# Self-attention on one core: the next queries' projection, the output projections and the norms in another order

## What is computed

```python
def _attn(xq, xc, Wq, Wk, Wv, Wo, bo):
    q = (xq @ Wq).reshape(B, N, HEADS, D_HEAD)      # 16 heads of 64
    k = (xc @ Wk).reshape(B, S, HEADS, D_HEAD)
    v = (xc @ Wv).reshape(B, S, HEADS, D_HEAD)
    scores = jnp.einsum('bnhd,bshd->bhns', q, k) * scale
    attn = jax.nn.softmax(scores, axis=-1)
    out = jnp.einsum('bhns,bshd->bnhd', attn, v).reshape(B, N, HEADS * D_HEAD)
    return out @ Wo + bo
...
x = _attn(_ln(x, g1, b1), _ln(x, g1, b1), Wq1, Wk1, Wv1, Wo1, bo1) + x
```

## Time and profile before

| | |
|---|---|
| median of 3 runs | 2309.28 us (2304.2 to 2310.44) |
| span of the profiled execution | 2302.8 us, 31305 instructions |
| self-attention in it, about | 571 to 1750 us |
| busy in the span | PE 92%, PEld 77%, DVE 70%, ACT 64%, POOL 46% |
| matmuls, 128x512, `mm3` | L146, L147, L148, 2944 each |
| exponentials L1500 | 256, mean 1027 ns |
| maxima L1588 | 256 of 1214 ns |

### The profile page before, as it was taken

The page is one execution under the profiler, slowest core; times in us unless marked ns, Lnnn a source line. Parts: engine busy times, 40 slices in busy tenths (PEclk is TensorE's granted clock), DMA queues, the critical chain, the costliest instruction groups (busy, mean ns, idle before and its releaser), DMA issues. The chain is left out here.

```text
span 2302.8 us, 31305 instructions
## 1 busy us (share of the span) xinstructions
PE 2128.1 (92%) x11628; PEld 1775.1 (77%) x11628; DVE 1608.6 (70%) x2345; ACT 1482.6 (64%) x2154; POOL 1070.1 (46%) x819
## 2 busy tenths in 40 slices
PE   7867999987799999999999999999998799999998
PEld 4656888876677778777777777777776689888987
DVE  5576676664677787777877778778776866666553
ACT  5546877754677777777777777777774345454431
POOL 2154444432245454454544545445444665656432
PEclk9989999999999999999999999999999999999999
DMA  6810000010100100100001000000004411111000
GB/s 219 290 40 4 22 22 21 10 67 28 33 24 15 33 15 15 38 15 24 24 15 33 15 24 29 15 33 15 24 26 152 144 46 56 56 56 47 10 10 19
DMA packets 84281, 102.67 MB, mean 45 GB/s; under 512 B 29665, under 2 KB 61153, under 8 KB 83617
## 3 DMA queue, kind: packets, MB, share of 16 engines
q1 hardware_dynamic: 84128, 100.66, 13.2%
HBM read 65.50 MB, written 33.82 MB: 43 GB/s over the span
## 5 line engine op out<-in xcount | busy, mean ns | idle before, releaser
L146 PE MATMUL PS<-R 128*128 128x512 f32 (+1 forms) x2944 | 1028.1, 349 | 84.0 <-DVE R L162 54.8
L148 PE MATMUL PS<-R 128*128 128x512 f32 (+1 forms) x2944 | 997.6, 339 | 0.0
L147 PE MATMUL PS<-R 128*128 128x512 f32 (+1 forms) x2944 | 997.3, 339 | 0.0
L146 PEld LDWEIGHTS PS<-R 128*128 128x128 f32 x2944 | 566.4, 192 | 197.5 <-DVE R L162 64.0
L156 ACT ACTIVATE R<-PS 64x512 fp32r<-64x512 f32 (+4 forms) x860 | 460.1, 548 | 238.7 <-PE PS L1805 129.4
L148 PEld LDWEIGHTS PS<-R 128*128 128x128 f32 x2944 | 565.7, 192 | 61.1
L147 PEld LDWEIGHTS PS<-R 128*128 128x128 f32 x2944 | 567.6, 193 | 54.8
L162 DVE TENSOR_TENSOR R<-F,R 128x1024 fp32r<-128x1024 f32 (+2 forms) x416 | 466.1, 1126 | 46.5 <-POOL R L159 23.2
L159 POOL TENSOR_SCALAR R<-F 128x1024 fp32r<-128x1024 f32 (+1 forms) x295 | 263.8, 896 | 292.6 <-DVE F L1958 149.3
L1500 ACT ACTIVATE F<-PS 128x1024 f32<-128x1024 f32 x256 | 263.0, 1027 | 172.7 <-DVE R L162 115.2
L159 POOL TENSOR_SCALAR R<-R 64x512 fp32r<-64x512 f32 x128 | 143.0, 1132 | 392.5 <-ACT R L156 392.4
(11 more groups left out here) (89 smaller groups left out, 1992.1 us busy)
## 6 DMA issues: line engine op xcount, KB each, us to landing
F<-sd SPq DMA_DIRECT2D x128, 128.0 KB, 2.8
xs<-F SPq DMA_DIRECT2D x16, 512.0 KB, 2.6
F<-xs SPq DMA_DIRECT2D x16, 512.0 KB, 3.6
gd<-F SPq DMA_DIRECT2D x8, 768.0 KB, 4.0
vd<-F SPq DMA_DIRECT2D x8, 768.0 KB, 6.3
R<-gd SPq DMA_DIRECT2D x6, 1024.0 KB, 5.6
R<-vd SPq DMA_DIRECT2D x6, 1024.0 KB, 5.7
F<-in_x SPq DMA_DIRECT2D x8, 512.0 KB, 5.4
```

The source lines that it names most:

```text
L146: nc.tensor.matmul(o, L[0], Rr[0], start=start, stop=False, skip_group_check=share)
L147: nc.tensor.matmul(o, L[0], Rr[1], start=False, stop=False, skip_group_check=share)
L148: return nc.tensor.matmul(o, L[1], Rr[0], start=False, stop=stop, skip_group_check=share)
```

## The change

Eight things are written in another place:

- `project(u + 1, 0)` stands in quarter 3 behind `values(d, 3)`, ahead of the transposes; it no longer waits for `o3_add`, since nothing else writes bank 2 behind the maxima. Only the very first one stays in quarter 0.
- `values(d, 0)` stands where `project(u, 0)` was, between the two parts of the first scores.
- `output(e, 0)` goes to bank 7 and stands behind the transposes, with a wait for all four maxima of the unit; `output(e, 1)` stays in bank 7, with a wait for the addition of half 0. The last pair keeps banks 4 and 5.
- On VectorE the probability rest of quarter 3 stands ahead of the addition of half 0.
- The load of the next batch's x, its statistics (`p = 3`), its scale and GpSimd's power (`p = 4`), and its transposes, weights and split (`p = 5`) all stand one unit earlier. GpSimd's `ln_add` stays behind `p = 5`.

```diff
--- before.py
+++ after.py
@@ -1272,7 +1272,7 @@
 
         def out3_bank(e, half):
 
-            return (4, 5)[half] if e == N3 - 1 else (2, 7)[half]
+            return (4, 5)[half] if e == N3 - 1 else 7
 
         def odd_bank(u):
 
@@ -1324,7 +1324,7 @@
                         sp_values(0)
                     for _ in range(early4.get(at, 0)):
                         next(ahead)
-                if ok(s, N3) and p == 3:
+                if ok(s, N3) and p == 2:
                     if b + 1 == NB:
                         sp_bias(3)
                     sp_load(*after3(b), xs)
@@ -1357,8 +1357,6 @@
                 pe.wait_ge(ln_nl, 17 + b)
                 wait_weights(pe, "q1", "k1")
                 pe.wait_ge(b3_max, 4 * (u - 1) + 2)
-                if n == 0:
-                    pe.wait_ge(o3_add, last_o3(u - 4))
                 for k in range(2):
                     m = mm3(bank(2 + n), [v[:, k, 128 * p:128 * p + 128] for v in (W3q, W3k)[n]],
                             [v[:, k, :] for v in ns[b % 2]], k == 0, k == 1)
@@ -1416,16 +1414,16 @@
             for s in loop3:
                 t, u, d = s, s + 1, s - 1
                 b, p = divmod(max(t, 0), 8)
-                norm = ok(t, N3) and p == 6
+                norm = ok(t, N3) and p == 5
                 for j in range(4):
                     if ok(t, N3):
                         scores(t, j, 0)
-                    if ok(u, N3) and j == 0:
+                    if u == 0 and j == 0:
                         project(u, 0)
+                    if ok(d, N3) and j == 0:
+                        values(d, j)
                     if ok(t, N3):
                         scores(t, j, 1)
-                    if ok(d, N3) and j == 0:
-                        values(d, j)
                     if ok(u, N3) and j == 0:
                         project(u, 1)
                     if ok(u, N3) and u > 0 and j == 1:
@@ -1444,21 +1442,23 @@
                         largest(u, 2 * j - 3, odd_bank(u))
                     if ok(d, N3) and j >= 2:
                         values(d, j)
+                    if ok(u + 1, N3) and j == 3:
+                        project(u + 1, 0)
+                    if ok(u, N3) and j == 3:
+                        pe.wait_ge(b3_max, 4 * u + 3)
+                        transposes(bank(odd_bank(u)), M3, 0).then_inc(nm3_mm.sem, 1)
                     e = s - 2 if j == 3 else s - 3
                     if j % 2 == 1 and ok(e, N3) and e % 2 == 1:
                         if j == 3:
-                            pe.wait_ge(b3_max, min(4 * u + 2, 4 * N3 - 1))
-                            pe.wait_ge(o3_add, e - 3)
+                            pe.wait_ge(b3_max, min(4 * u + 3, 4 * N3 - 1))
+                            pe.wait_ge(o3_add, e - 2)
                             if e == N3 - 1:
                                 pe.wait_ge(d3_out, e)
                             output(e, 0, out3_bank(e, 0))
                         else:
                             pe.wait_ge(b3_max, min(4 * u - 1, 4 * N3 - 1))
-                            pe.wait_ge(o3_add, e - 2)
+                            pe.wait_ge(o3_add, e - 1 if e < N3 - 1 else e - 2)
                             output(e, 1, out3_bank(e, 1))
-                    if ok(u, N3) and j == 3:
-                        pe.wait_ge(b3_max, 4 * u + 3)
-                        transposes(bank(odd_bank(u)), M3, 0).then_inc(nm3_mm.sem, 1)
                     if u == 0 and j == 3:
                         project_v(u)
                     if ok(u, N3) and j in (1, 2):
@@ -1552,7 +1552,7 @@
                         value(u)
                     for _ in range(early4.get(tail3(s, j), 0)):
                         next(ahead)
-                    if j == 2 and ok(t, N3) and p == 6:
+                    if j == 2 and ok(t, N3) and p == 5:
                         ln_affine(18 + b, *((P_G1, P_B1) if b + 1 < NB else (P_G2, P_B2)), 6)
                     if s < 0:
                         yield s
@@ -1624,7 +1624,7 @@
                     if u == 0 and j == 3:
                         value(u)
                     e = s - 2 if j == 3 else s - 3
-                    if j in (1, 2) or j == 3 and not (ok(e, N3) and e % 2 == 1):
+                    if j > 0:
                         rests(4 * s + j - 1)
                     if j % 2 == 1 and ok(e, N3) and e % 2 == 1:
                         half = int(j == 1)
@@ -1635,19 +1635,17 @@
                             dve.wait_ge(o3_add, e - 3 + half)
                         nc.vector.tensor_tensor(xv, bank(out3_bank(e, half)).rearrange("p (a c) -> p a c", a=2), xv, ALU.add
                                                 ).then_inc(o3_add.sem, 1)
-                        if j == 3:
-                            rests(4 * s + 2)
                     if ok(u, N3) and j in (1, 2):
                         largest(u, 2 * j - 2, 2)
                     for job in weights3_at(s, j):
                         dve_weight_rest(job)
                     for _ in range(early4.get(tail3(s, j), 0)):
                         next(ahead)
-                    if more and j == 3 and p == 4:
+                    if more and j == 3 and p == 3:
                         ln_x_stats(*after3(b))
                     if s < 0:
                         yield s
-                if more and p == 5:
+                if more and p == 4:
                     ln_scale(18 + b, xbuf(*after3(b)), C)
             for _ in ahead:
                 pass
@@ -1708,10 +1706,10 @@
                         pool_weight(job)
                     for _ in range(early4_pool.get(tail3(s, j), 0)):
                         next(ahead)
-                    if j == 2 and more and p == 6:
+                    if j == 2 and more and p == 5:
                         pool.wait_ge(v3_mm, 8 * (b - 1) + 7)
                         ln_split_pool(18 + b, ns[(b + 1) % 2])
-                    if more and j == 0 and p == 5:
+                    if more and j == 0 and p == 4:
                         ln_pool_rstd(18 + b)
                     if s < 0:
                         yield s
```

## The result

The changed kernel takes 2316.02 us (median of 20 runs, 2311.86 to 2319.27), the kernel before 2308.16 (20 runs): 1.0033 times as long, interval 1.0025 to 1.0040, so 7.9 us slower. I had forecast slower, by 14.4 us, with 2324 as the time. The sign and the mechanism of the steady steps came out, the size did not: it is hardly more than half of the sum. The profiled execution has a span of 2313.2 us, 10.4 more than that of before.

The account below looks back on a forecast made before the run. Even steps were taken as bound by a VectorE, TensorE and ScalarE chain, odd ones as becoming TensorE-bound; 12 us (odd steps) plus 2.4 (norms) on 2309.28 gave 2323.7 us, forecast's own range 2316 to 2332, overall range 2300 to 2334.

Parts of the forecast that it names:

- Even step: Self-attention's even steps: TensorE's waits close, but ScalarE's copies still hold the end; value 0, at best 0.1 us per step.
- the one that I named: Even step's chain: first exponential, copies, VectorE's rests, addition, TensorE's quarters 2 and 3, ScalarE's eight copies; 18.54 us.
- Odd step: Self-attention's odd steps: TensorE releases the next exponential later; 0.4 us each in 30 steps, 12 us.
- Norms: Norm parts move from even to odd steps: 2.1 us per norm instead of 1.8, 2.4 us more in all.
- The faster rival: Closing TensorE's gaps shortens 31 even steps by 1.36 us each: 42 us less, 2267 us; chance 0.18.
- The sum: Whole kernel: odd steps' 12 us plus norms' 2.4 us make 14.4 us on 2309.28, so 2323.7 us.
- the first steps: Start of self-attention, where weights are still loaded: with the last steps, only 2 us in the range, nothing in the sum.

Follow-up runs that it names:

- x4: Changed kernel with VectorE's addition of output half 1 one instruction earlier in even steps, ahead of the rest of probability block 0: 2316.7 us, 1.0039 times the kernel before.
- x2: Changed kernel with values(d, 0) moved back behind the second part of the first scores in every step: 2292.9 us, 0.9933 times the kernel before.
- x9: Changed kernel with output(e, 0) back ahead of the maxima's transposes: 2319.0 us, 1.0054 times the kernel before.
- x7: Kernel before with only the norm's seven parts one unit earlier: 2309.4 us, 1.0008 times the kernel before.
- x8: x3 with VectorE's last probability rest ahead of the queries' rests and GpSimd's copy of block 0 ahead of the keys' copies: 2272.3 us, 0.9844 times the kernel before.
- x3: Changed kernel with values(d, 0) behind the second part of the first scores only where an even step begins: 2291.5 us, 0.9929 times the kernel before.
- x6: Changed kernel with queries' projections of units 0 to 3 and the values' product of steps 0 to 2 in old places: 2320.8 us, 1.0058 times the kernel before.

## Why the prediction was right and wrong

*Even step.* Right in each point: no wait ahead of the transposes, values(d, 0) waits for the copies out of banks 4 and 5, the step's length stays (18.54 before and 18.53 after), TensorE waits in front of `largest` instead. What I did not see is that a second chain ends only 0.3 us ahead of the one that I named (x4).

*Odd step.* Right: 0.38 us more by the trace, 0.4 forecast. x2 shows the cause, the six matmuls ahead of the second part of the scores; x9 rules out the output projection's place.

*Norms.* Right: 2.19 us above its like instead of 1.82; x7 has 2.13. Forecast were 2.1 against 1.8.

*The faster rival* is refuted by the even steps. The waits it wanted to save were saved, and the even steps from 3 to 63 did not become shorter. The rule of the Trainium skill that I weighed there (Perfetto Trace Analysis, Optimization Strategy: find the gaps of the most-contended engine and let what they wait for start sooner) does not hold for this case as a way to read off a gain: the longest of its waits was closed, and the time rose by 8 us. x8 moved nothing on TensorE against x3, only on VectorE and GpSimd, and won 19.

*The sum.* This is the step that failed: "14.4 us on 2309.28" took the cost of the steady steps for the whole, and the term that was mis-sized is that of the first steps. Steps 3 to 63 cost 13.3 us, near enough, though the parts differ a little: 30 odd steps at 0.38 are 11.5 where I had 12, the norms 3.0 where I had 2.4, and the even steps, by their means, gave back about 1.3 where I had 0. The first steps, which I had put into the range as 2 us of either sign with a middle of nought, gave 2.1 us back in all three traces. The sum had no reason for the nought: 0.6 of them are the queries' projection, for which ScalarE waited 1.5 us at the end of step 0, which stands in ScalarE's timeline of the trace before and from which I drew nothing; 1.3 are TensorE's clock, which was at its lower level behind a wait of 3.00 us (x6). That leaves 11.2. (The base of the sum, the median of three runs, lies 1.1 us above the median of twenty; that is a part of the miss in the total, not in the difference.)

The remaining 2 to 3 us between that and the runs stay open. The first comparison (1.0025 to 1.0040, so 5.8 to 9.2 us) excludes 11.2, the second (1.0033 to 1.0058, 7.6 to 13.4) includes it. All 75 executions of the kernel before have a mean of 2307.6 us and all 26 of the changed one 2316.3: 8.7 us. The spans of the traces alone give 11.4 (means 2301.9 and 2313.3). A run's time lies 1.8 us above its span, so these are times of 2303.7, which is 3.9 below the mean of all, and 2315.1, 1.1 below. So the three traces of the kernel before are faster than is usual for it. Since self-attention repeats within 1 us, the missing time must lie outside it, where the traces of the kernel before spread from 1135.6 to 1143.3 us; their mean (1139.9, against 1140.1 in the changed kernel) can't tell 3 us. Whether the change wins something there, or chance does, no trace shows.

## To carry to other kernels

A gap on the busiest engine costs only what the step's end costs; follow back what starts the next step, on whatever engine, before you count the gap as a gain. Where work is moved into a gap, look at what now stands in front of the instruction that releases the next engine: here six matmuls there cost 1.0 us in every second step. The steady loop is not the whole sum: its start has waits of its own, and a long wait of TensorE can cost a second time by the clock behind it (1.3 us in step 0). And work whose inputs are long ready belongs into the time in which its engine waits anyway (x8).

## What the runs showed of the hardware

The stretches in which TensorE's granted clock is at its lower level (1.2 GHz) differ from one execution of the same kernel to the next: 0.89, 0.94 and 0.93 on the mean in the 120 us behind step 63 in three traces of the kernel before, and step 63 to the end then took 556.2, 553.1 and 550.5 us. In self-attention most of the steps 3 to 62 repeat to 0.05 us in the three traces of a kernel; the worst differs by 0.46.

A rest on VectorE (line 162, 128x1024) takes 1.22 us where GpSimd does nothing beside it (1076.75 in step 26 of the changed kernel) and more where GpSimd's subtraction (line 165) runs. VectorE's and then GpSimd's row in the changed kernel, and GpSimd's row in x4, where the rest from 1081.54 took 2.14 us:

```profile
1080.74 1.84 DVE L162 TENSOR_TENSOR R<-F,R 128x1024 fp32r<-128x1024 f32 x1
1080.20 1.29 POOL L165 TENSOR_TENSOR R<-F,R 128x512 fp32r<-128x512 f32 x1
```

```profile
1081.31 1.30 POOL L165 TENSOR_TENSOR R<-F,R 128x512 fp32r<-128x512 f32 x1
```

With 0.75 us of the subtraction beside it the rest took 1.84 us, with 1.07 us it took 2.14; both ended some 1.1 us behind the subtraction. The Trainium skill (GPSIMD Engine Reference, Key points) says that GpSimd shares its SBUF interfaces with VectorE and that VectorE's instructions with two SBUF inputs contend; these rows agree.
